# Gated output in single chunks behind three gate banks, and an inverse root in seven operations instead of nine

## What is computed

```
h = layernorm(x) * (1 + ca) + sa                    # "LN0"
x = x + ga * attention(h)                           # 8 heads, causal, latent keys and values
h = layernorm(x) * (1 + cb) + sb                    # "LN1"
x = x + gb * experts0(h)                            # 8 experts of 64, 2 chosen per token
h = layernorm(x) * (1 + ca) + sa                    # "LN2"
x = x + ga * scan_mixer(h)                          # convolution, state scan over the tokens
h = layernorm(x) * (1 + cb) + sb                    # "LN3"
x = x + gb * experts1(h)                            # 8 experts of 512, 2 chosen per token

layernorm(x) = (x - mean(x)) / sqrt(var(x) + 1e-5)
experts0:  hmid = gelu(einsum('th,eih->tei', x, w_fc))
           y    = einsum('tei,ehi->teh', hmid, w_proj)
           out  = einsum('teh,te->th', y, gates)
```

## Time and profile before

| what | value |
| --- | --- |
| median of 3 runs | 1444.25 us |
| lowest and highest | 1441.99 and 1444.91 us |
| the profiled execution, its own time | 1446.64 us |
| its span, first to last instruction | 1445.1 us |
| mean granted TensorE clock, share of full | 0.947 |
| PE busy | 1213.7 us, 84% |
| PE weight loads busy | 763.6 us, 53% |
| DVE busy | 1072.1 us, 74% |
| ACT busy | 866.7 us, 60% |
| POOL busy | 462.5 us, 32% |

### The profile page before, as it was taken

How to read it: one execution, slowest core, us unless ns; L and a number is a source line. 1 busy time by engine, 2 the same in 40 slices (tenths; PEclk the granted TensorE clock), 3 DMA queues, 4 the chain that set the end, 5 groups by cost and what they waited for, 6 DMA issues and landing times. The chain is left out here.

```text
span 1445.1 us, 23043 instructions
## 1 busy us (share of the span) xinstructions
PE 1213.7 (84%) x6560; PEld 763.6 (53%) x6560; DVE 1072.1 (74%) x2491; ACT 866.7 (60%) x1608; POOL 462.5 (32%) x276
## 2 busy tenths in 40 slices
PE   5974689878898889978898888988899889888697
PEld 4641155545554556545556465645556456555465
DVE  2656977699767897589876997679875998579711
ACT  2625355586547866488555866488664876378342
POOL 0003910096003830068100950048200770039300
PEclk8986589999999999999999999999999999999899
DMA  6102100020002100020001200021000300011000
GB/s 234 67 16 74 44 8 8 24 102 1 16 16 75 44 16 2 16 90 30 16 10 44 82 1 16 16 75 44 16 2 16 102 15 9 1 63 56 7 1 8
DMA packets 18545, 53.68 MB, mean 37 GB/s; under 512 B 4960, under 2 KB 5848, under 8 KB 18016
## 3 DMA queue, kind: packets, MB, share of 16 engines
q1 hardware_dynamic: 16112, 43.40, 9.3%
q0 software_dynamic: 1280, 4.20, 1.0%
q10 hardware_dynamic: 1008, 4.38, 0.8%
HBM read 45.40 MB, written 2.38 MB: 33 GB/s over the span
## 5 line engine op out<-in xcount | busy, mean ns | idle before, releaser
L1396 DVE TENSOR_TENSOR_SCAN probs_T<-bank,probs_T 128x512 f32<-128x512 f32 x256 | 304.9, 1212 | 40.8 <-ACT bank L997 28.5
L435 POOL TENSOR_TENSOR probs_T<-step_space,probs_T 128x1024 f32<-128x1024 f32 x120 | 281.8, 2357 | 0.0
L556 PEld LDWEIGHTS bank<-w_w,hidden 128*128 128x128 f32 x2048 | 243.4, 192 | 65.7 <-issue 62.0
L544 PE MATMUL bank<-hT,w_w 128*128 128x512 f32 x512 | 256.2, 620 | 16.8 <-ACT hidden L852 16.8
L556 PE MATMUL bank<-w_w,hidden 128*128 128x128 f32 x2048 | 247.4, 276 | 9.7 <-DVE step_space L1378 6.2
L852 ACT ACTIVATE hidden<-bank,w_b 128x512 f32<-128x512 f32 x256 | 171.1, 686 | 133.5 <-PE bank L544 132.3
L433 POOL TENSOR_TENSOR probs_T<-step_space,probs_T 128x512 f32<-128x512 f32 x16 | 22.4, 1417 | 700.2 <-DVE step_space L1386 700.2
L925 ACT ACTIVATE probs<-bank,row_neg 128x128 f32<-128x128 f32 (+3 forms) x256 | 135.0, 528 | 166.8 <-DVE row_neg L1247 147.6
L997 ACT ACTIVATE bank<-step_space,a_neg 128x512 f32<-128x512 f32 x256 | 168.4, 683 | 71.0 <-DVE probs_T L1396 62.0
L1247 DVE TENSOR_REDUCE row_neg<-bank 128x1 f32<-128x128 f32 (+3 forms) x256 | 122.6, 485 | 91.4 <-PE bank L640 86.1
L638 PE MATMUL bank<-k_pad,q_lat 128*128 128x512 f32 (+3 forms) x512 | 185.5, 449 | 5.4 <-DMA k_pad<-xc 5.4
(11 more groups left out here) (174 smaller groups left out, 1591.8 us busy)
## 6 DMA issues: line engine op xcount, KB each, us to landing
probs_T<-b_rows_dram SPq DMA_DIRECT2D x64, 512.0 KB, 3.7
w_w<-in_w_dram ACTq DMA_DIRECT2D x2, 2048.0 KB, 13.3
k_pad<-xc SPq DMA_DIRECT2D x64, 64.0 KB, 2.0
x_in<-in_x_dram POOLq DMA_DIRECT2D x8, 256.0 KB, 3.3
gate<-gate_rows_dram SPq DMA_DIRECT2D x1, 2048.0 KB, 7.3
out_dram<-x_out POOLq DMA_DIRECT2D x8, 256.0 KB, 2.9
step_space<-in_wmod_dram SPq DMA_DIRECT2D x1, 768.0 KB, 5.8
probs_T<-in_wqT_dram SPq DMA_DIRECT2D x1, 512.0 KB, 4.0
```

Of the source, the lines that this page charges most:

```text
L435: ins = nc.gpsimd.tensor_tensor(inject[:, n % 3, :, :], u[:], row.unsqueeze(1).to_broadcast([P, DH, T]), ALU.mult)
L544: mm(hid1_bank(n)[:], w["w1"][:, n // C1, n % C1 * P:(n % C1 + 1) * P], hT[3][:], start=True, stop=True).then_inc(hid1_mm.sem, 1)
L556: ins = mm(bank[OUT1_BANK[e]][:, t * P:(t + 1) * P], hidden[:, (e * C1 + c) % (2 * C1), t * P:(t + 1) * P], w["w2"][:, e * C1 + c, :], sta ...
L1396: v.tensor_tensor_scan(state[:, n % 2, c, :], decay(DH * n + c)[:], inject[:, n % 3, c, :], 0.0, ALU.mult, ALU.add).then_inc(st_ok.sem, 1)
```

## The change

The gate banks become banks 0, 4, 5 and 0 again. Banks 4 and 5 are those of the hidden chunks, so the turns of chunks 1 and 2 wait for the GELUs of chunks 2 and 3, which read these banks last; chunk 3 goes into bank 0, after PE's wait for chunk 0 to be gated. The output matmuls go chunk by chunk, all four chunks summing into bank 6, with the start flag on the first matmul alone: turn 0, turn 1, output 0, turn 2, turn 3, output 1, 2, 3, each output behind a wait for its own gated chunk. The two expert hiddens between the turns move behind the output matmuls, where the other two of that expert stand; on ACT all four GELUs come after the values are taken.

The inverse root takes another guess, one Newton step with fitted constants (three operations, the scale ROOT_S left in) and one third-order step (four operations): seven operations instead of nine. NORM_STEPS goes from 14 to 12, LN3's steps fill units 8 to 13 instead of 8 to 14, LN0's start at unit 22 instead of 21.

```diff
@@ -46,7 +46,8 @@
 PR = 3 * BC + NS
 EPS = 1e-5
 SCALE = float(P) ** -0.5
-ROOT_GUESS = float(0x5F3759DF)
+ROOT_GUESS = float(0x5F1FFFF9)
+ROOT_A, ROOT_B, ROOT_S = 0.703952253, 2.38924456, 0.375
 FAR = -3.0e38
 
 
@@ -191,7 +192,7 @@
 
 
         bank = [ctx.enter_context(nc.psum_tensor(f"bank{i}", [P, T], F32)) for i in range(8)]
-        C_BANK, HID0_BANK, GATE_BANK, OUT_BANK, MISC = 1, (4, 5), (0, 6), 6, 7
+        C_BANK, HID0_BANK, GATE_BANK, OUT_BANK, MISC = 1, (4, 5), (0, 4, 5, 0), 6, 7
         SUM_BANK = 7
         PRE_BANK = 1
         DECAY_BANK = (4, 5, 0)
@@ -729,24 +730,33 @@
                     mm(bank[HID0_BANK[c % 2]][:], w["wfcT"][:, c * P:(c + 1) * P], hT[1][:], start=True, stop=True
                        ).then_inc(hid0_mm.sem, 1)
                 pe.wait_ge(gates_ok.sem, gates_ok.at(b, 1))
-                for c in range(C0):
-                    if c == 2:
-                        early(1, (0, 1))
-                    if c >= 2:
-                        pe.wait_ge(hid0_gate.sem, hid0_gate.at(b, c - 1))
+
+                def turn_gates(c):
                     for t in range(NT):
                         wide = gates_wide[:, t, :, :].rearrange("p e f -> p (e f)")
-                        ins = tr(bank[GATE_BANK[c % 2]][:, t * P:(t + 1) * P], wide[:, c * P:(c + 1) * P], ident[:])
+                        ins = tr(bank[GATE_BANK[c]][:, t * P:(t + 1) * P], wide[:, c * P:(c + 1) * P], ident[:])
                     ins.then_inc(gT_mm.sem, 1)
-                pe.wait_ge(hid0_gate.sem, hid0_gate.at(b, C0))
-                for t in range(NT):
-                    for c in range(C0):
+
+                def out0(c):
+                    pe.wait_ge(hid0_gate.sem, hid0_gate.at(b, c + 1))
+                    for t in range(NT):
                         ins = mm(bank[OUT_BANK][:, t * P:(t + 1) * P], gated[:, c, t * P:(t + 1) * P],
-                                 w["wprojT"][:, c, :], start=(c == 0), stop=(c == C0 - 1))
+                                 w["wprojT"][:, c, :], start=(c == 0 and t == 0), stop=(c == C0 - 1), skip_group_check=True)
+                    return ins
+
+                turn_gates(0)
+                pe.wait_ge(hid0_act.sem, hid0_act.at(b, 3))
+                turn_gates(1)
+                out0(0)
+                pe.wait_ge(hid0_act.sem, hid0_act.at(b, 4))
+                turn_gates(2)
+                turn_gates(3)
+                for c in range(1, C0):
+                    ins = out0(c)
                 ins.then_inc(out0_mm.sem, 1)
                 if ahead:
                     project(b + 1, 4)
-                early(1, (2, 3))
+                early(1, (0, 1, 2, 3))
                 if behind and ahead:
                     pe.wait_ge(v_out.sem, v_out.at(b + 1, 1))
                 early(0, out=True)
@@ -1119,10 +1128,13 @@
                 link(ts(var_eps[:], meanvar[:, :, 1], EPS, None, ALU.add))
 
                 link(ts(rstd[:].bitcast(I32), var_eps[:].bitcast(I32), -0.5, ROOT_GUESS, ALU.mult, ALU.add))
-                for _ in range(3):
-                    link(tt(newton[:], rstd[:], rstd[:], ALU.mult))
-                    link(stt(newton2[:], newton[:], -0.5, var_eps[:], ALU.mult, ALU.mult))
-                    link(stt(rstd[:], newton2[:], 1.5, rstd[:], ALU.add, ALU.mult))
+                link(tt(newton[:], rstd[:], rstd[:], ALU.mult))
+                link(stt(newton2[:], newton[:], -ROOT_A * ROOT_S, var_eps[:], ALU.mult, ALU.mult))
+                link(stt(rstd[:], newton2[:], ROOT_A * ROOT_B * ROOT_S, rstd[:], ALU.add, ALU.mult))
+                link(tt(newton[:], rstd[:], rstd[:], ALU.mult))
+                link(stt(newton2[:], newton[:], ROOT_S ** -2, var_eps[:], ALU.mult, ALU.mult))
+                link(stt(newton[:], newton2[:], -10.0 / 3.0, newton2[:], ALU.add, ALU.mult))
+                link(stt(rstd[:], newton[:], 5.0, rstd[:], ALU.add, ALU.mult))
                 for t in range(NT):
                     ins = ts(xn[:, t, :], x[:, t, :], meanvar[:, t, 0:1], rstd[:, t:t + 1], ALU.subtract, ALU.mult)
                 ins.then_inc(of(ln_xn, j), 1)
@@ -1186,12 +1198,17 @@
                     ins = ts(var_eps[:], meanvar[:, :, 1], EPS, None, ALU.add)
                 elif k == 3:
                     ins = ts(rstd[:].bitcast(I32), var_eps[:].bitcast(I32), -0.5, ROOT_GUESS, ALU.mult, ALU.add)
-                elif k in (4, 7, 10):
+                elif k in (4, 7):
                     ins = tt(newton[:], rstd[:], rstd[:], ALU.mult)
-                elif k in (5, 8, 11):
-                    ins = stt(newton2[:], newton[:], -0.5, var_eps[:], ALU.mult, ALU.mult)
-                elif k in (6, 9, 12):
-                    ins = stt(rstd[:], newton2[:], 1.5, rstd[:], ALU.add, ALU.mult)
+                elif k in (5, 8):
+                    by = -ROOT_A * ROOT_S if k == 5 else ROOT_S ** -2
+                    ins = stt(newton2[:], newton[:], by, var_eps[:], ALU.mult, ALU.mult)
+                elif k == 6:
+                    ins = stt(rstd[:], newton2[:], ROOT_A * ROOT_B * ROOT_S, rstd[:], ALU.add, ALU.mult)
+                elif k == 9:
+                    ins = stt(newton[:], newton2[:], -10.0 / 3.0, newton2[:], ALU.add, ALU.mult)
+                elif k == 10:
+                    ins = stt(rstd[:], newton[:], 5.0, rstd[:], ALU.add, ALU.mult)
                 else:
                     for t in range(NT):
                         ins = ts(xn[:, t, :], x[:, t, :], meanvar[:, t, 0:1], rstd[:, t:t + 1], ALU.subtract, ALU.mult)
@@ -1342,7 +1359,7 @@
                 for c in range(C0):
                     dve.wait_ge(hid0_act.sem, hid0_act.at(b, c + 1))
                     dve.wait_ge(gT_mm.sem, gT_mm.at(b, c + 1))
-                    tt(gated[:, c, :], hid0[:, c, :], bank[GATE_BANK[c % 2]][:], ALU.mult).then_inc(hid0_gate.sem, 1)
+                    tt(gated[:, c, :], hid0[:, c, :], bank[GATE_BANK[c]][:], ALU.mult).then_inc(hid0_gate.sem, 1)
                 dve.wait_ge(out0_mm.sem, out0_mm.at(b, 1))
                 add_mixed(b, 1, bank[OUT_BANK][:].rearrange("p (t d) -> p t d", d=P), x, out0_add, link)
                 dve.wait_ge(out0_add.sem, out0_add.at(b, 1))
@@ -1429,10 +1446,10 @@
 
 
 
-CHAIN = {"tail": 4, "attend": 19, "main": 37, "head": 16, "act main": 4}
-NORM_STEPS = 14
-NORM_UNITS = 7
-PRE_UNIT = 21
+CHAIN = {"tail": 4, "attend": 17, "main": 35, "head": 16, "act main": 4}
+NORM_STEPS = 12
+NORM_UNITS = 6
+PRE_UNIT = 22
 ALL_BY_ACT = 12
 LAG = 3
 LAST_SUM, LAST_READ, PE_MIXER, DVE_MIXER, FINISH, TAKE_X, NORM_UNIT = 3, 2, 6, (3, 7), 5, 8, 8
```

## The result

| what | before | after |
| --- | --- | --- |
| median | 1443.18 us (6 runs, 1441.54 to 1447.32) | 1428.56 us (6 runs, 1422.70 to 1432.78) |
| ratio of the times | | 0.9886, 95% interval 0.9864 to 0.9908 |
| the profiled execution | 1446.64 us, span 1445.1 | 1432.78 us, span 1431.2 |
| its mean granted clock | 0.947 | 0.944 |

The change makes the kernel 1.1% faster. Forecast were 10.2 us less in the profiled execution; it took 13.9 less.

What follows compares the result with a forecast made beforehand. PE's own queue was taken as the bound up to LN2 in batches 1 to 7. Gains of 2.45 + 1.2 + 6.6 = 10.2 us took the profiled 1446.64 to 1436.4, the median to 1434.0; eight-in-ten range 1428 to 1441.

Steps and rivals of the forecast that it cites:

- LN3: Norm inside the attention: 0.3 us of 0.39 gained, seven times, 2.1 us; bounds 0 and 0.39.
- Gate part: Gate turns and output matmuls, batches 1 to 7: 7.96 us against 8.31, 0.35 us less per batch, 2.45 over seven.
- Batch 0: Gate part of the first batch, without covering hiddens: 7.24 us before, 6.05 after, 1.2 us less.
- LN2: Norm behind the gate part: 0.39 us less in batch 0, nothing in batches 1 to 7, hidden by 1.5 us to spare.
- LN1: Norm ahead of the router: 0.3 us less in batches 1 to 6, 0.39 in batches 0 and 7, 2.6 us together.
- LN0: Norm in the attention's second half: perhaps 0.1 us less, seven times, 0.7 us; bounds 0 and 0.39.
- the 0.39 at the start: First norm at the kernel's start, where nothing else runs: two operations fewer, 0.39 us less.
- The 0.20 us an operation: Small chained DVE operations of the inverse root: 0.20 us start to start, so two fewer save 0.39 us per norm.
- The ring: Rival, gate part: later output groups each wait some 0.5 us, batches 1 to 7 lose 10.5 us; 1444.5 us, chance 0.07.
- The clock: Rival, gate part: TensorE's clock falls, 5.5 us more per batch; 1478 us if all eight lose it, chance 0.06.
- The attention hides its part: Rival, attention: its chain passes by the small operations, so 2.8 us of the gain go; 1436.8 us, chance 0.12.
- its opposite: Rival: attention gives all of its gain and the run of four hiddens does not stall; 1428 us, chance 0.05.

Runs made afterwards that it cites:

- root_only: The kernel before with only the new inverse root and its schedule of steps, without the gate part's change: 1432.46 us, ratio 0.9912.
- t2_first: The changed kernel with LN2's turn on PE and modulation on ACT moved ahead of expert hiddens 8 and 9, batches 1 to 7: 1414.3 us, ratio 0.9797.

## Why the prediction was right and where it was wrong

**Direction and time.** Forecast 1434.0 us, measured 1428.56: faster, as said, but by more. That is below the forecast's own range of 1430 to 1438.5, and at the low edge of the wide one, 1428 to 1441; by the ratio of 0.9886 the 1444.25 us of the kernel before become 1427.8, just outside it. (The prediction calls a second range its own, 1427.2 to 1439.4, the bounds of the sum.) The gain in the profiled pair was forecast as 10.2 us and measured as 13.9, some 1.3 of it in batch 7 and not the change's. What made the sum too small is the term of LN3, below.

**Gate part, right.** The first group was forecast 1.44 us after the first turn and stands at 1.43; the next three do not wait; mixed comes 2.33 us earlier (2.3 said); the run of four hiddens takes 3.84 us (3.79 said). The sum was 0.35 a batch and is 0.41. Batch 0: 1.2 forecast; from the first turn to the end of the output it is 7.23 us before and 5.99 now, 1.24 less. Only 1.0 shows behind the gates' copy, because the first turn comes 0.24 later after that copy, behind a projection that took 1.83 us instead of 1.59.

**LN2, right.** 0.39 us in batch 0, nothing in the others, shown by root_only; t2_first then took up the slack that hides it.

**LN1, right in sum for the wrong reason.** "I take 0.3" of the 0.39. The two operations gave the full 0.39 to xn's chain, but in batches 2 to 6 a pause of 0.28 us came to stand ahead of xn: LN1's turn gained 0.11. The router behind it, for which nothing was forecast, gained 0.33 in batches 2 to 5 by a pause that left it. That the two make up for each other is luck.

**LN3, the step that failed.** "Bounds 0 and 0.39": the upper bound was the two operations' own time, although the same paragraph had seen xn and maximum 15 change places. The move of a 1.1 us operation out of the chain, into time that DVE waited anyway, has a price of its own, and the sum had no term for it. Measured: 0.36 for the place, 0.23 for the operations, some 0.24 for a pause that left the second choice, 0.84 to 1.03 a batch in all, in place of 0.3. Over the kernel the attention gave 5.6 us where 2.1 for LN3 and 0.7 for LN0 stood in the sum.

**LN0, wrong in size.** "Perhaps 0.1" a batch; it is nothing. Nor do the 0.39 at the start arrive: x is taken 0.02 us earlier.

**The 0.20 us an operation, right.** LN2's chain is 0.38 to 0.40 us shorter for two operations in each of the eight batches. By the 60 ns of the Trainium skill, "Perfetto Trace Analysis", section "Optimizing Scalar/DVE Operations", weighed in the prediction, an estimated 0.13.

**The rivals.** The ring does not wait further down. The clock does not fall in the gate part: PEclk is 1.00 in batch 3. So the rule of the Trainium skill, "TensorE: Matmul & The Clock Gate", section "A second HAM failure mode: psum-queue depth-cycling", does not show itself at a wait of 0.34 us. "The attention hides its part" was the wrong side: it gave more than its part, and nearly the 1428 of its opposite, though not by that rival's terms. Two of the rivals were sized loosely: the full 0.39 in the attention and no stall come to 14.2 us by the prediction's own terms, so 1430 and not 1428; and the low clock's 5.5 us a batch doubles the 5.54, where 1.11 against 0.60 would give 4.7.

## What to carry to other kernels

When an edit removes steps from a hand-laid schedule, price the moves apart from the removals: ask for each long operation whether it left a chain and landed in a wait. Where an engine reaches a result long after it is ready, its own queue is the bound, and swapping two entries of that queue (1.4 us a batch here) is worth more than shortening what feeds it (nothing here). When single medians swing by more than the effect, compare the same stretch in two traces: outside the attention and the scan that settled 0.03 us here, while times did not settle 4.

## What the runs showed of the hardware

Where DVE's stream steps from one block of 128 instructions to the next inside a chain of dependent operations, DVE paused for 0.24 to 0.35 us in every trace here, and in the four traces read for it an 8 KB packet on an instruction queue followed. Added or removed DVE instructions move the later pauses: fourteen memsets at the start moved 0.33 us into the router of each of five batches and 0.35 into their scan's end. A small change in a chained kernel can therefore bring a gain or loss of this size that has nothing to do with its purpose.
